# Routing of the second mixture of experts moved into the attention before it, for 14 of 16 token tiles

## What is computed

```python
def _layernorm(x, axis=-1, eps=1e-05):
    m = jnp.mean(x, axis=axis, keepdims=True)
    v = jnp.var(x, axis=axis, keepdims=True)
    return (x - m) / jnp.sqrt(v + eps)

    x = x + _L1_xattn_ref(_layernorm(x, axis=-1), ctx_2048, mask_BxS2_bk0)
    x = x + _L1_ffn_ref(_layernorm(x, axis=-1), L1_ffn_router_w, L1_ffn_gate_w, L1_ffn_up_w, L1_ffn_down_w)

    # _L1_xattn_ref: softmax(x @ memory.T / 16, masked) @ memory, 1601 memory rows per batch
    # _L1_ffn_ref:
        route = jax.nn.sigmoid(x @ router_w)
        max_ind = jnp.argmax(route, axis=1)
        max_prob = jnp.take_along_axis(route, max_ind[:, None], axis=1)
        for e in range(num_experts):
            mask = (max_ind == e)[:, None]
            h = jax.nn.silu(x @ gate_w[e]) * (x @ up_w[e])
            out = out + jnp.where(mask, h @ down_w[e], 0.0)
        out = out * max_prob
```

## Time and profile before

| | us |
|---|---|
| median of 3 runs (2922.61 to 2924.23) | 2923.95 |
| the profiled execution | 2918.47 |
| its span, first to last instruction | 2916.6 |
| PE busy / DVE / ACT / POOL | 2780.5 / 2052.8 / 1974.1 / 1697.1 |
| mean granted clock of PE | 0.975 of full |

### The profile page before, as it was taken

How to read it: one execution, slowest core, us unless ns; L and a number is a source line. 1 busy time by engine, 2 the same in 40 slices (tenths; PEclk the granted TensorE clock), 3 DMA queues, 4 the chain that set the end, 5 groups by cost and what they waited for, 6 DMA issues and landing times. The chain is left out here.

```text
span 2916.6 us, 57647 instructions
## 1 busy us (share of the span) xinstructions
PE 2780.5 (95%) x18157; PEld 2443.6 (84%) x18157; DVE 2052.8 (70%) x4824; ACT 1974.1 (68%) x4918; POOL 1697.1 (58%) x2124
## 2 busy tenths in 40 slices
PE   7989999799999999999999999999999997699698
PEld 5768888699999999999999999999999984499655
DVE  7974454577777777777777777777777758866444
ACT  5656666677777777777777777777777747666211
POOL 6766663365665665665666666556656537387122
PEclk9999999899999999999999999999999989899699
DMA  5447767612111111211111111121111014464510
GB/s 181 134 145 213 209 206 206 205 43 71 56 43 61 52 56 43 70 56 43 70 51 48 48 66 56 43 71 56 43 64 49 15 50 91 120 195 131 191 37 27
DMA packets 284601, 263.44 MB, mean 90 GB/s; under 512 B 46382, under 2 KB 260527, under 8 KB 284304
## 3 DMA queue, kind: packets, MB, share of 16 engines
q1 hardware_dynamic: 264784, 238.94, 25.8%
q10 hardware_dynamic: 17312, 15.73, 1.9%
q0 software_dynamic: 2208, 5.12, 0.6%
HBM read 167.34 MB, written 84.93 MB: 86 GB/s over the span
## 5 line engine op out<-in xcount | busy, mean ns | idle before, releaser
L1030 ACT ACTIVATE w_hi<-ps_t 128x512 fp32r<-128x512 f32 (+2 forms) x1024 | 568.4, 555 | 352.3 <-PE ps_t L1273 343.8
L1132 DVE TENSOR_TENSOR w_lo<-ps_t,w_hi 128x512 fp32r<-128x512 f32 (+2 forms) x1024 | 655.7, 640 | 178.8 <-ACT w_hi L1030 175.4
L1106 DVE TENSOR_REDUCE piece_max<-ps_s 128x1 f32<-128x512 f32 (+1 forms) x768 | 472.2, 622 | 238.2 <-PE ps_s L1260 221.6
L1293 PE MATMUL ps_o<-w_hi,v_hi 128*128 128x256 f32 (+1 forms) x1856 | 596.4, 321 | 0.0
L1203 POOL TENSOR_SCALAR prob<-prob,inv_sum 128x512 f32<-128x512 f32 (+2 forms) x768 | 477.8, 641 | 189.2 <-DVE inv_sum L1122 189.2
L1295 PE MATMUL ps_o<-w_hi,v_lo 128*128 128x256 f32 (+1 forms) x1856 | 523.6, 282 | 0.0
L1294 PE MATMUL ps_o<-w_lo,v_hi 128*128 128x256 f32 (+1 forms) x1856 | 522.3, 281 | 0.0
L1273 PE MATMUL ps_t<-ident,prob 128*128 128x128 f32 (+1 forms) x2784 | 517.8, 273 | 0.0
L1273 PEld LDWEIGHTS ps_t<-ident,prob 128*128 128x128 f32 (+1 forms) x2784 | 356.7, 140 | 62.8 <-DVE w_lo L1132 8.7
L1258 PE MATMUL ps_s<-k_hi,q_hi 128*128 128x512 f32 (+2 forms) x1024 | 395.9, 387 | 10.2 <-PEq L57 4.8
L1259 PE MATMUL ps_s<-k_lo,q_hi 128*128 128x512 f32 (+2 forms) x1024 | 377.6, 369 | 0.0
(11 more groups left out here) (288 smaller groups left out, 6352.3 us busy)
## 6 DMA issues: line engine op xcount, KB each, us to landing
v_scratch<-v_out SPq DMA_DIRECT2D x120, 256.0 KB, 3.0
raw_k<-k_scratch SPq DMA_DIRECT2D x32, 960.0 KB, 7.0
raw_v<-v_scratch SPq DMA_DIRECT2D x32, 960.0 KB, 4.7
k_scratch<-k_out SPq DMA_DIRECT2D x104, 256.0 KB, 2.7
q_scratch<-out_t SPq DMA_DIRECT2D x64, 256.0 KB, 2.5
r_all<-r_scratch SPq DMA_DIRECT2D x32, 512.0 KB, 4.2
raw_q<-q_scratch SPq DMA_DIRECT2D x32, 512.0 KB, 5.2
first_prob<-in_ctx_t ACTq DMA_DIRECT2D x50, 256.0 KB, 2.8
```

The costliest lines, as they stand in the source:

```text
L1030: nc.scalar.activation(pt_hi[keys, k % RING, cols], ps_t[keys, k % 2, cols], ACT.Copy).then_inc(hi_done, 1)
L1106: nc.vector.tensor_reduce(piece_max[:, n % 2, p:p + 1], ps_s[:, p, lo - p * PC:hi - p * PC], AX.X, ALU.max).then_inc(max_ready, 1)
L1132: nc.vector.tensor_tensor(pt_lo[keys, k % RING, cols], ps_t[keys, k % 2, cols], pt_hi[keys, k % RING, cols].bitcast(F32), ALU.subtract).th ...
L1293: nc.tensor.matmul(out, v_hi[gi][keys, vs], pt_hi[keys, k % RING, cols], start=blk == (0 if qt else 1), stop=False)
```

## The change

- Tiles 0 to 13 (`EARLY_ROUTED`) are measured, normalised, turned, multiplied with the router and given their best expert inside the second attention. For tile t: DVE `measure` in slot 1 of tile t+1; POOL `root_next` at the end of tile t+1; DVE `normalise_next` in slot 0 of tile t+2; PE `turn_half` ahead of the transposes of pieces 1 and 2, and `route_next` ahead of those of piece 0, into free columns of `ps_t`; ACT `copy_half` and `score_exponential` ahead of `high`; DVE `choose` for two tiles in slot 2 of every even tile from 6 on. Tiles 12 and 13 are turned and routed at the end of the attention, in the memory of the scores.
- The sigmoid becomes 1/(1+exp(-x)), by ACT's exponential and DVE's reciprocal.
- Mean, variance and inverse deviation are written behind each row of `x_rows`, whose rows grow from 256 to 259 numbers. Three DMAs of 12-byte pieces do that: two on SP at the end of the attention (12 and 2 tiles), one on ACT in the routing block (2 tiles). The gather then brings them with the row.
- Token number and score go through the one-hot matmul as five bf16 pieces that add up exactly; `in_slot`, `in_lane`, `own` and `facts` are bf16, the matmuls too. The splitting of the score is five small operations on POOL. `facts` grows from 1472 to 1840 elements.
- The router is loaded in the attention block; PE waits for each of the three weights where it first needs it.

The diff, cut to its core:

```diff
+EARLY_ROUTED = NT - 2
...
+def stats_of(x_rows, first, end):
+    return x_rows[first * P:end * P, D:D + ROW_STATS].rearrange("(t p) n -> p t n", p=P)
...
+                for first, end in ((0, STORED), (STORED, EARLY_ROUTED)):
+                    sp.wait_ge(rooted, end)
+                    sp.dma_start(stats_of(x_rows, first, end), next_mean_var[:, first:end, :]).then_inc(rows_written, 16)
...
+                def root_next(t):
+                    pool.wait_ge(measured, t + 1)
+                    nc.gpsimd.tensor_scalar(var_eps[:, t:t + 1], next_mean_var[:, t, 1:2], LN_EPS, 1.0, ALU.add, ALU.mult).then_inc(eps_added, 1)
+                    pool.wait_ge(eps_added, t + 1)
+                    nc.gpsimd.tensor_tensor(next_rstd[:, t:t + 1], var_eps[:, t:t + 1], half[:, 0:1], ALU.pow).then_inc(rooted, 1)
...
+                        if 0 <= i * UB + u - 1 < EARLY_ROUTED:
+                            root_next(i * UB + u - 1)
...
+                def copy_half(n, c):
+
+                    t, half_at = n - 3, c - 1
+                    act.wait_ge(next_xt_ready, 2 * t + c)
+                    if t >= 2:
+                        act.wait_ge(logits, t - 1)
+                    nc.scalar.activation(next_xt[:, t % 2, half_at, :], ps_t[:, (n * SL + c) % 2, AT:AT + P], ACT.Copy).then_inc(next_xt_copied, 1)
+
+                def score_exponential(n):
+
+                    act.wait_ge(logits, n - 3)
+                    nc.scalar.activation(score_exp[:, n - 4, :], ps_t[:, (n * SL) % 2, AT:AT + E1], ACT.Exp, scale=-1.0).then_inc(score_exps, 1)
+
...
+                    if c in (1, 2) and 0 <= i * UB + u - 3 < TAIL:
+                        copy_half(i * UB + u, c)
+                    if c == 0 and 0 <= i * UB + u - 4 < TAIL:
+                        score_exponential(i * UB + u)
...
+                def measure(t):
+                    dve.wait_ge(x_added, t + 1)
+                    nc.vector.bn_stats(stats[:, t, :], x_sb[:, t, :]).then_inc(stats_ready, 1)
+                    dve.wait_ge(stats_ready, t + 1)
+                    nc.vector.bn_aggr(next_mean_var[:, t, 0:2], stats[:, t, :]).then_inc(measured, 1)
+
+                def normalise_next(t):
+                    dve.wait_ge(rooted, t + 1)
+                    if t >= 3:
+                        dve.wait_ge(next_xt_ready, 2 * (t - 2))
+                    nc.vector.tensor_scalar(next_xn[:, t % 3, :], x_sb[:, t, :], next_mean_var[:, t, 0:1], next_rstd[:, t:t + 1],
+                                            ALU.subtract, ALU.mult).then_inc(next_xn_ready, 1)
+                def choose(g):
+                    two = slice(2 * g, 2 * g + 2)
+                    dve.wait_ge(score_exps, 2 * g + 2)
+                    nc.vector.tensor_scalar(score_den[:, two, :], score_exp[:, two, :], 1.0, None, ALU.add).then_inc(score_dens, 1)
+                    dve.wait_ge(score_dens, g + 1)
+                    nc.vector.reciprocal(score[:, two, :], score_den[:, two, :]).then_inc(scored, 1)
+                    dve.wait_ge(scored, g + 1)
+                    for t in (2 * g, 2 * g + 1):
+                        nc.vector.max(best[:, t, :], score[:, t, :]).then_inc(maxed, 1)
+                    for t in (2 * g, 2 * g + 1):
+                        dve.wait_ge(maxed, t + 1)
+                        nc.vector.max_index(best_at[:, t, :], best[:, t, :], score[:, t, :]).then_inc(indexed, 1)
 
...
+                                if 0 <= i * UB + u - 1 < EARLY_ROUTED:
+                                    measure(i * UB + u - 1)
+                            if s == 0 and 0 <= i * UB + u - 2 < EARLY_ROUTED:
+                                normalise_next(i * UB + u - 2)
+                            if s == 2 and u % 2 == 0 and i * UB + u >= 6:
+                                choose((i * UB + u - 6) // 2)
+                            if s == 2 and i * UB + u == NT - 1:
+                                choose(TAIL // 2 - 1)
...
+                    if c in (1, 2) and 0 <= i * UB + u - 3 < TAIL:
+                        turn_half(i * UB + u - 3, c - 1, ps_t[:, k % 2, AT:AT + P]).then_inc(next_xt_ready, 1)
+                    if c == 0 and 0 <= i * UB + u - 4 < TAIL:
+                        route_next(i * UB + u - 4, ps_t[:, k % 2, AT:AT + E1]).then_inc(logits, 1)
...
+                def turn_half(t, c, out):
+
+                    pe.wait_ge(next_xn_ready, t + 1)
+                    return nc.tensor.transpose(out, next_xn[:, t % 3, c * P:c * P + P], ident[:, :])
+
+                def route_next(t, out):
+
+                    if t == 0:
+                        pe.wait_ge(router_loaded, 16)
+                    pe.wait_ge(next_xt_copied, 2 * t + 2)
+                    for c in range(DC):
+                        last = nc.tensor.matmul(out, next_xt[:, t % 2, c, :], router[:, c, :], start=c == 0, stop=c == DC - 1)
+                    return last
+
+                def turn_tail(t):
+                    pe.wait_ge(max_ready, NT * SL)
+                    for c in range(DC):
+                        last = turn_half(t, c, ps_s[:, t % 2, c * P:c * P + P])
+                    last.then_inc(next_xt_ready, 2)
+
...
+                            if s == 2 and i * UB + u >= TAIL + 2:
+                                turn_tail(i * UB + u - 2)
+                            if s == 3 and i * UB + u >= TAIL + 2:
+                                route_next(i * UB + u - 2, ps_s[:, 2 + u % 2, 0:E1]).then_inc(logits, 1)
...
+TOKEN_PARTS, SCORE_PARTS = 2, 3
+PARTS = TOKEN_PARTS + SCORE_PARTS
+ROW_STATS = 3
+STORED = 12
...
+                act.wait_ge(rooted, 1)
+                act.dma_start(stats_of(x_rows, EARLY_ROUTED, NT), mean_var[:, late, :]).then_inc(rows_written, 16)
+                act.wait_ge(xt_ready, 1)
+                nc.scalar.activation(xt[:, :], ps_t[:, :], ACT.Copy).then_inc(xt_copied, 1)
+                act.wait_ge(logits, 1)
+                nc.scalar.activation(score_exp[:, :, :], ps_l[:, :].rearrange("p (t e) -> p t e", t=LATE), ACT.Exp, scale=-1.0).then_inc(score_exps, 1)
...
+                nc.gpsimd.tensor_tensor(rstd[:, late], var_eps[:, :], half[:, 0:LATE], ALU.pow).then_inc(rooted, 1)
...
+                value, parts = best[:, :, 0], [own[:, :, TOKEN_PARTS + n] for n in range(SCORE_PARTS)]
+                nc.gpsimd.tensor_copy(parts[0], value).then_inc(part_made, 1)
+                pool.wait_ge(part_made, 1)
+                nc.gpsimd.tensor_tensor(rest[:, 0, :], value, parts[0], ALU.subtract).then_inc(part_made, 1)
+                pool.wait_ge(part_made, 2)
+                nc.gpsimd.tensor_copy(parts[1], rest[:, 0, :]).then_inc(part_made, 1)
+                pool.wait_ge(part_made, 3)
+                nc.gpsimd.tensor_tensor(rest[:, 1, :], rest[:, 0, :], parts[1], ALU.subtract).then_inc(part_made, 1)
+                pool.wait_ge(part_made, 4)
+                nc.gpsimd.tensor_copy(parts[2], rest[:, 1, :]).then_inc(own_set, 1)
...
-                nc.vector.tensor_copy(fact[:, :, :], ps_f[:, :].rearrange("p (n s) -> p n s", n=FACTS)).then_inc(fact_ready, 1)
+                nc.vector.tensor_reduce(fact[:, 0, :], ps_f[:, 0:TOKEN_PARTS, :].rearrange("p n s -> p s n"), AX.X, ALU.add).then_inc(fact_ready, 1)
...
-        xg = sb("xg7", [P, RING, D])
+        xg = sb("xg7", [P, RING, D + ROW_STATS])
...
+                        if s == 0:
+                            pe.wait_ge(w_loaded[0 if w is gate_w else 1], 16)
...
-                    nc.vector.tensor_scalar(xn[:, s % 2, :], xg[:, s % RING, :], fact[:, 1, s:s + 1], fact[:, 2, s:s + 1],
+                    nc.vector.tensor_scalar(xn[:, s % 2, :], xg[:, s % RING, 0:D], xg[:, s % RING, D:D + 1], xg[:, s % RING, D + 2:D + 3],
...
-                    nc.vector.scalar_tensor_tensor(made[:, s % RING, :], ps_y[:, s % 2, 0:D], fact[:, 3, s:s + 1], xg[:, s % RING, :],
+                    nc.vector.scalar_tensor_tensor(made[:, s % RING, :], ps_y[:, s % 2, 0:D], fact[:, 1, s:s + 1], xg[:, s % RING, 0:D],
...
-        moe_slots(nc, x_rows, (rows_written, 16 * NT), (gate_sb, up_sb, down_sb), out_dram.rearrange("b l d -> (b l) d"),
-                  ident, read_at, write_at, fact, expert_of, (w_loaded, 3 * 16))
+        moe_slots(nc, x_rows, (rows_written, 16 * (NT + 3)), (gate_sb, up_sb, down_sb), out_dram.rearrange("b l d -> (b l) d"),
```

193 lines of the change are left out of this document (112 added, 81 removed).

## The result

The changed kernel takes 2930.02 us in the median (2924.6 to 2942.72, 11 runs) against 2922.73 (2918.44 to 2924.23, 11 runs) for the kernel before on the same chips: ratio 1.0031, 95% interval 1.002 to 1.0043. Forecast were 2913 and a range of 2906 to 2924. Slower by 0.3% was the one thing that only the last rival foresaw.

What follows compares the result with a forecast made beforehand. PE was taken to bound attention and slots, a serial chain the routing block. Routing -23.7, PE work +7.8, waits +3.0, attention's end +0.9 and first gather +1.3 made -10.7 us: 2923.95 to 2913, range 2906 to 2924.

Steps and rivals of the forecast that it cites:

- the last rival: Third rival: DVE sets the attention's pace at `transpose_x`, all new work end to end, 2.9 us a tile, 2943; chance 0.08.
- Attention, waits: Attention: PE's added waiting for DVE and ACT, before `transpose_x` and behind the mask, +3.0 us (0 to 7).
- The old wait of 0.18: PE's existing idle time before `transpose_x`, waiting for `add_x`; forecast change 0 (-0.2 to +0.3 us a tile).
- The first paragraph: What bounds the kernel: PE in the attention, the slots PE-bound, a serial chain of 46.7 us in the routing block.
- stalls behind the mask: PE waiting for a late `xt_lo` before slot 0's products: three times 0.87 us and 0.35 at tile 2.
- PE's work: Attention: two transposes and two f32 router matmuls add 0.59 us a tile, +7.8 us in all (6.5 to 13).
- the second rival: Dearer PE rows: the router's rows cost 0.215 us at full clock too, +5.6 us, 2919; chance 0.12.
- Routing block: Serial chain before the first gather: head 20.0 us shorter, tail 3.9 shorter, a reduction +0.2; together -23.7 (22 to 25).
- End of the attention: After the last product: router rows, exponential and `choose` take 1.9 us against 1.0 before, +0.9 us.
- The first gather: After the routing block: it now runs while weights still load, so it lands later, +1.3 us (0 to 4).
- The first rival: The weights starve the gathers: the first gather waits for everything queued before it, +10 us, 2923; chance 0.12.
- both milder rivals: Starved gathers (2923) and dearer PE rows (2919), chance 0.12 each; named as the range's high end, 2924.

Runs made afterwards that it cites:

- e1: Changed kernel with `normalise_next` subtracting the mean with an accumulator, the deviation applied as scale of ACT's exponential: 2914.32 us, 0.9967 of the kernel before.
- e2: Changed kernel without `normalise_next` in the attention: PE turns x itself, router columns centred once, deviation in ACT's exponential: 2910.46 us, 0.9953 of the kernel before.
- e6: Changed kernel without `normalise_next`, with the last two tiles in the routing block also turned straight from x: 2903.93 us, 0.9942 of the kernel before.
- e11: The kernel of e6 run again, unchanged: 2903.05 us, 0.9942 of the kernel before.
- e8: Kernel before with rows of 259 numbers in the scratch of x and in the gathers: 2924.9 us (one run).
- e7: The kernel of e6 with the down weights' load issued only after the first two gathers have landed: 2907.71 us, 0.9951 of the kernel before.
- e5: Kernel before plus one DVE operation from SBUF to SBUF with constant scalars, in slot 0 of 14 tiles: 2924.46 us, 1.0011 of the kernel before.

## Why the prediction was wrong, point by point

**The step that failed** is in "Attention, waits": "DVE's `normalise_next` (0.4) stands ahead of slot 1", and with it "The old wait of 0.18 stays about as it is: 0" and the term 3.0 (0 to 7). The 0.4 is right for the operation alone (0.42). In its place it took 1.96 to 3.79 us in twelve of fourteen tiles, because it waited until POOL's operation had ended, and that wait passed through `add_x` to PE (18.6 us of idle time before `transpose_x`); a tile of the first thirteen took 13.2 us on average (2729.18 - 2570.74 over 12 intervals), 10.7 before. The first paragraph prepared the mistake: "new work of DVE or ACT is free as long as PE does not come to wait for it", with DVE's idle 13.5 us as the reserve. POOL's 34.11 of 40 us was checked for POOL's own new work only ("so nothing"), not as the time in which DVE may be shut out.

**The rival that came true** is the third, at the place it named, `transpose_x` behind `add_x`. It said that it decides from 1.5 us a tile and that from 1.95 the kernel is slower; measured was 2.5 a tile over those twelve intervals. Its price, 2.9 a tile and 2943, was built from the wrong parts (all new work end to end, 0.45 for `normalise_next`): that 2.9 a tile lies near the measured 2.5 is luck, and 2943 is 13 us too high. Its chance, 0.08, rested on "DVE idles 13.5 of 40 us", which is no argument: DVE was busy for only 27.08 of 40 when it happened. The waiting is inside the operation's duration, and the chain is serial.

**The other waits.** The forecast stalls behind the mask, 0.87 in tiles 7, 9 and 11 and 0.35 at tile 2, are missing in the changed kernel, in which `penalty` took 0.98 to 1.13 us. In e1 PE sat idle before products of slot 0 for 1.05 us each in just those three tiles (3.2 in all; nothing at tile 2). The place is as forecast and the size near it, but not for the reason given: the forecast took 0.95 for all five steps of `choose`, and the first of them was again an operation that waited for POOL, with 16 elements a partition:

```profile
2632.66 1.87 POOL L1934 TENSOR_TENSOR r_lo<-raw_r,r_hi 128x768 fp32r<-128x768 f32 x1 [1.20 <-ACT r_hi L1984]
2633.71 0.85 DVE L2172 TENSOR_SCALAR score_den<-score_exp 128x16 f32<-128x16 f32 x1
```

It took 0.83 to 0.85 in those tiles and 0.17 where POOL was idle, and `penalty` took 2.66 to 2.69 ahead of it. In e2 and e6 the stall came only in the tiles in which `penalty` took 3.07 or 3.10 and not 1.25 to 1.27: two tiles in e2, one in e6 (1.04), none in e11, the same kernel as e6. The old wait before `transpose_x` did not stay; behind more PE work it vanished (0.2 us in e2). That the sum in e1, 11.7, is so near the forecast 10.8 is in part luck.

**PE's work**, 0.59 us a tile: right. In e6 a tile in the steady part takes 11.15 us (2604.56 to 2626.86 over two); before it took 10.73, of which 0.18 was that wait. 11.15 - 10.55 = 0.60. So the second rival (rows at 0.215 at full clock, which makes 1.0) fell.

**Routing block**, -23.7 forecast: -24.2. Head: `best_f` after 8.0 us, 8.25 forecast; the power of two columns 0.70, as taken. Tail: `facts` 2.07 (2.0); `fact` straight behind `expert_of`; POOL's pieces of the score were done at 2758.7, 4.7 us ahead of `facts`.

**End of the attention**, +0.9: +0.6. **The first gather**, +1.3 (0 to 4): it landed 2.4 later, inside its range; e8 and e7 put it down to the weights, as the term had it. By the prediction's estimate from "DMA: Bandwidth & Descriptors" (the Trainium skill, section on queues, rings and completion order) it would have been 0.6; the run shows four times that. The first rival, gathers that wait for all the weights (+10), fell: they land while the weights run. The slots: +0.4, 0 forecast. The upper end of the range, 2924, is called both milder rivals; added up they give 2929 (2913 + 10 + 5.6), and the measured median lies beyond that too.

With -24.2 + 30.9 + 0.6 + 2.6 + 0.4 the change comes to +10.3 in the traces (the medians of all runs differ by 7.3), and 1.1 us ahead of the attention is not the change's (first `add_x` stood anywhere from 2569.2 to 2576.9 in these runs). One term was far off, the waits in the attention, by about 19 us. e1, with the wait of `normalise_next` removed, gains 9.9 us on the kernel before beside it (2924.26 to 2914.32), where 10.7 was forecast.

## What to carry to other kernels

Before an operation is added to DVE beside a busy POOL, look at its form: one source in SBUF, result in SBUF is the form that waited until POOL's instruction had ended in these runs, even with 16 elements a partition, unless it came just ahead of that instruction (e5); a source in PSUM, or the form with an accumulator, took the same time whatever POOL did. An operation whose mean in the trace is several times its minimum (0.98 and 2.72 us for `penalty`) is such a wait, even where it costs nothing yet; ask for minimum and maximum, not the mean, and lay POOL's rows beside it. And ask first whether the operation is needed: a mean can be taken out of the weights and a deviation put into the next activation's scale, which was worth 2.9 us of attention more than the form that does not wait.
